# Expert slots in half pairs (68 positions for 71, eight of them split), a slot list in lines of 64 bytes, and routing done a step sooner

## The chip, the cores and the metric

The kernel runs on one core of one Trainium2 chip. The metric is device microseconds (us) from launch to end, the median of several executions. Engines are named as the profile names them: PE (matrix products), PEld (its weight loads), DVE (elementwise work on vectors), ACT (activation functions), POOL (here mostly the issuer of gathers and scatters), SP (an issuer of DMAs). Each engine runs its own instruction list in order and waits on semaphores.

## The reference, cut to what matters

```python
xn = layernorm(x)                                  # x: 2 x 4096 tokens x 256, float32
# deformable attention: 16 heads, 12 samples a query, offsets from a small convolution
g   = gelu(depthwise_conv3(xn @ wq.T + bq))
pos = clip(token + anchor + 6 * tanh(g @ pw_w.T + pw_b), 0, 4095)
k_at, v_at = linear_sample(k, pos), linear_sample(v, pos)
s   = softmax(q . k_at / 4 - rel_scale * |pos - token|) . v_at @ wo.T + bo
# mixture of 8 experts, the best 2 for each token, hidden width 512
p   = softmax(xn @ Wr.T + br);  best 2 of (scores + biases_N), weights p / sum(p of the two)
h   = xn @ Wl1[e] + bl1[e]                         # 256 -> 1024, halves a and b
y_e = (silu(a) * b) @ Wl2[e] + bl2[e]              # 512 -> 256
out = x + s * silu(sum over the two e of weight_e * y_e)
```

8192 tokens with two experts each make 16384 rows of expert work. They are sorted by expert into slots; an expert's last slots may stay empty (they point at rows of zeros behind the tokens).

## The kernel before, in words

**Front** (`front_block`, about 0 to 367 us). First layernorm, V and router scores, tile by tile. Then 16 steps of 512 tokens. In a step PE runs `head_scores` (products of q with nearby keys, four tiles), `project` (q and k of two steps ahead) and `offsets` (the offset products of one step back, two halves into one PSUM tile `pOff`). ACT evacuates, does gelu and tanh and stores. DVE runs `convolve`, `slopes_of_k`, `offset_bias` (frees `pOff`) and `positions`.

Beside the steps DVE does the routing: `choose` (best two) in step 0, `gate_values` and `count_rows` in step 1, `find_slots` and `experts_of_pairs` in step 2; PE's `count_tokens` (sums over tokens) stands at the end of step 1. `find_slots` gives the place of each (token, choice) in a slot list in DRAM. POOL writes that list by 128 indirect DMAs (`scatter`, L556), each 128 elements of 4 bytes, and between their quarters clears the 8 MB that experts add into (`clear_moe`, four DMAs of 2 MB) and loads two experts' first weights (`first_w1`). At the end POOL reads the list back, DVE turns it into token numbers (`inv`, L1157 and L1158), and POOL gathers the first token rows with them.

**Experts** (`mix_block`, to about 1182 us). 71 pairs, each of 2 x 128 slots of one expert. In `period(n)` PE runs `times_w1` twice (into `pA` and `pB`, L1670), `transpose_x` of the next pair (L1664), and `products` of the pair two back (L1723, L1676). ACT applies silu to `pA`, evacuates `pB` and the output. DVE multiplies the two (`gate_hidden`, L1790) between its own 16 steps of attention weights; tables say where (`GATES_AT`), and after which pair or tile ACT does each softmax exponent and its preparation (`EXPONENT_AFTER`, `PREPARE_AFTER`, `END_EXPONENT_AT`, `END_PREPARE_AT`). POOL's `pair_io(n)` loads the weights of pair n+2 (three slots, the third is the tile `bandT`), gathers that pair's token rows (L1379), and `take_y` adds results into DRAM by two scatters (L1398); the scatters of a pair wait for those of the pair before to have landed.

**Tail** (to the end). 64 tiles of 128 tokens: PE transposes bands of attention weights (L1689), multiplies by V (L1704) and by wo (L1714, L1715); SP loads bands, ACT's queue loads V, POOL loads expert sums and writes the output; ACT's `gate_unit` (silu of expert sums) stands at tiles of `END_GATE_AT`, DVE's units of the output at `UNITS_AT` and after the last step. DVE finishes its last steps of attention weights beside it; each of the 16 steps is stored as `band_rows` and feeds four tiles.

Of the kernel before, what the change touches and what calls it, by code (L numbers as in the profile page):

```python
# [30 lines left out]
P = 128  # L31
F32 = mybir.dt.float32
BF16 = mybir.dt.bfloat16
I32 = mybir.dt.int32
# [25 lines left out]
SLOT_PAIRS = TOKENS * TOPK // (2 * P) + EXPERTS - 1  # L60
# [5 lines left out]
LISTED = TOPK * TILES  # L66
COUNT_AT = 1
# [49 lines left out]
STAGE_AT = XS_AT = 2 * KT_PITCH  # L117
ACT_AT = XS_AT + XS_F
# [14 lines left out]
GATES_AT = ((0, 2, 3, 4, 6, 7), (0, 2, 3, 5, 6, 8), (1, 2, 4, 5, 7), (0, 1, 3, 4, 6, 7), (0, 2, 3, 5, 6, 8), (0, 2, 4, 5, 6),  # L133
            (0, 1, 2, 4, 6, 7), (0, 1, 3, 4, 6, 7), (0, 2, 3, 5, 6, 8), (1, 2, 4, 5, 7), (0, 1, 3, 4, 6, 7), (0, 2, 3, 4, 6, 8), (0, 2))
EXPONENT_AFTER = (0, 6, 12, 17, 23, 29, 35, 40, 46, 52, 57, 63, 69)
PREPARE_AFTER = (3, 8, 14, 20, 26, 31, 37, 43, 48, 54, 60, 66)
END_EXPONENT_AT = (6, 24, 42)
END_PREPARE_AT = (1, 14)
END_GATE_AT = (5, 9, 13, 17, 22, 25, 29, 33, 37, 41, 45, 49, 53, 56, 58, 60)
UNITS_AT = ({}, {}, {2: 1, 4: 1, 6: 1}, {0: 1, 2: 1, 4: 1, 6: 1}, {4: 1, 6: 1, 7: 1})  # L140
# [3 lines left out]
def anchors():  # L144

    step = np.arange(SAMPLES, dtype=np.float32) * np.float32(1.0 / (SAMPLES - 1))
    a = np.float32(-RHO) * (np.float32(1) - step) + np.float32(RHO) * step
    a[-1] = RHO
    return [float(v) for v in a]

# [95 lines left out]
def front_block(nc, io, dram, keep):  # L246


    with ExitStack() as ctx:
# [51 lines left out]
        ones = sb("ones", [P, P])  # L301
        rows_i = sb("rows_i", [P, EXPERTS], I32)
        rows = sb("rows", [P, EXPERTS])
        ends = sb("ends", [P, EXPERTS])
        start = sb("start", [P, EXPERTS])
        slot = sb("slot", [P, TOPK, TILES])
        tile_row = sb("tile_row", [1, SLOT_PAIRS])
        tile_exp = sb("tile_exp", [1, SLOT_PAIRS])
        list_f = sb("list_f", [P, HIGH])
        spare_i = sb("spare_i", [P, HIGH], I32)  # L310
        token_i = sb("token_i", [P, TOPK * TILES], I32)
        slot_i = sb("slot_i", [P, TOPK, TILES], U32)
# [26 lines left out]
        pOff = ps("pOff", [P, 512])  # L339
        pCount = ps("pCount", [P, 2 * EXPERTS])  # L340
# [7 lines left out]
        pads_set = sem("pads_set")  # L348
        consts = sem("consts")
# [37 lines left out]
        prefix_ready = sem("prefix_ready")  # L387
        list_set = sem("list_set")
        list_rows = sem("list_rows")
# [3 lines left out]
        keep["front_sx_stored"], keep["front_pads_set"] = sx_stored, pads_set  # L393
        keep["front_stored"] = [(pos_stored[u], 16 * SUBS * (STEPS // 2)) for u in range(2)] + [(sx_stored[u], 16 * STEPS) for u in range(SX_SLOTS)]
        keep["front_stored"] += [(pads_set, 16 * 9), (gates_stored, 16 * 4), (bias_stored, 16)]
# [4 lines left out]
        TAIL = VROWS - TOKENS - REACH  # L400
        HALVES = SUBS // 2
        WEIGHTS = 16 * 7
        ROUTE_WEIGHTS = WEIGHTS + 16 * 5
        CONSTS = 8
# [18 lines left out]
        step = keep["step"]  # L423
        assert XST_AT <= SEQ + 2 and FREE_SLOTS * PAIRS <= SEQ + 2 and PARTS_AT >= XST_AT + KC * PAIR + 3 * TH
# [3 lines left out]
        def _(sp):  # L428
# [94 lines left out]
        def _(pool):  # L523
# [15 lines left out]
            nc.gpsimd.iota(keep["tile_exp"][:], pattern=[[PAIR, SLOT_PAIRS]], base=0, channel_multiplier=0).then_inc(consts, 1)  # L539
# [7 lines left out]
            pool.dma_start(dram["list"].rearrange("(p n) o -> p (n o)", p=P), spare_i[:]).then_inc(list_set, 16)  # L547
# [5 lines left out]
            pool.wait_ge(list_rows, 1)  # L553
# [1515 lines left out]
```

## Time and profile before

| | |
|---|---|
| median of 3 runs | 1437.6 us (1434.17 to 1440.89) |
| the profiled execution | 1440.41 us |
| its span (first to last instruction) | 1438.7 us |
| busy: PE / DVE / ACT / POOL | 1356.0 / 1223.1 / 802.4 / 861.8 us |
| mean granted TensorE clock | 0.976 of full |

A row of a timeline is: start, length, engine, line, operation, output<-inputs, count, and in brackets the idle time before it with what ended it. PE's fp32 matmul shows as two passes: 8 instructions of the program are "x16". A row of windows gives each engine's busy time in a stretch, the granted clock and the share of the DMA engines. Busy is not bound: an engine bounds a stretch where it has no idle time in it or where the others' waits end with it.

### The profile page before, as it was taken

How to read it: one execution, taken by the hardware profiler on the slowest of the kernel's cores; microseconds unless marked ns; L12 is line 12 of the kernel's file. 1: busy time of each engine (PE TensorE's matmuls, PEld its weight loads, DVE VectorE, ACT ScalarE, POOL GpSimd, SP SyncE). 2: the span in 40 equal slices, each digit the busy share in tenths (PEclk: the TensorE clock that was granted, in tenths of full speed). 3: DMA queues.
4: the chain of work that ended last, by engine and by line, in shares of the span. 5: the costliest groups of instructions: out<-in, count | busy, mean ns of one | idle time of the engine just before them, and what ended most of it. 6: DMA issues, size and time to landing. Idle time of an engine off the chain costs nothing. (4 is left out here: it accounts for less than half of the span.)

```text
span 1438.7 us, 35852 instructions
## 1 busy us (share of the span) xinstructions
PE 1356.0 (94%) x13687; PEld 1085.2 (75%) x13687; DVE 1223.1 (85%) x1700; ACT 802.4 (56%) x1873; POOL 861.8 (60%) x566
## 2 busy tenths in 40 slices
PE   5998999997799999999999999999999998899997
PEld 4864565556688888888888888888888886777775
DVE  7846755786899999999999999999999999999361
ACT  2547577777445455545444555545454455665664
POOL 1000377887568888778787877988887746121021
PEclk9999899998899999999999999999999999999999
DMA  7942456886747687775768577677767678999798
GB/s 226 348 166 88 105 161 201 252 258 211 250 134 214 173 233 192 224 225 150 242 141 256 142 229 192 169 223 176 212 153 214 167 169 268 250 267 228 217 275 170
DMA packets 204278, 293.98 MB, mean 204 GB/s; under 512 B 25601, under 2 KB 161029, under 8 KB 203891
## 3 DMA queue, kind: packets, MB, share of 16 engines
q0 software_dynamic: 65792, 146.59, 39.9%
q1 hardware_dynamic: 110723, 133.04, 29.3%
q10 hardware_dynamic: 27632, 12.64, 3.5%
q8 instruction: 79, 1.29, 0.4%
q14 instruction: 52, 0.43, 0.1%
HBM read 182.83 MB, written 117.74 MB: 209 GB/s over the span
## 5 line engine op out<-in xcount | busy, mean ns | idle before, releaser
L1398 POOL DMA_INDIRECT moe_rows<-expert_mem,token_of x142 | 363.3, 2558 | 90.3 <-issue 49.9
L1676 PE MATMUL pY<-expert_mem 128*128 x1136 | 264.2, 386 | 0.0
L1379 POOL DMA_INDIRECT expert_mem<-xn_rows,token_of x138 | 227.7, 1650 | 52.5 <-issue 45.1
L1676 PEld LDWEIGHTS pY<-expert_mem 128*128 128x128 f32 x1136 | 210.0, 190 | 41.8 <-issue 16.1
L1867 DVE SCALAR_TENSOR_TENSOR mid<-pos_pair,mid 128x768 f32<-128x768 f32 x224 | 197.6, 954 | 0.5
L1670 PE MATMUL pA<-mid,expert_mem 128*128 128x256 f32 x768 | 177.4, 385 | 4.4 <-ACT mid L1504 2.7
L1523 ACT ACTIVATE expert_mem<-pA,b1sel 128x256 f32<-128x256 f32 x284 | 111.2, 474 | 122.9 <-issue 122.7
L556 POOL DMA_INDIRECT slot_list<-token_i,high_part x128 | 141.0, 1101 | 58.2 <-issue 38.7
L1670 PE MATMUL pB<-mid,expert_mem 128*128 128x256 f32 x768 | 173.6, 379 | 0.0
L1532 ACT ACTIVATE expert_mem<-pB,b1sel 128x256 f32<-128x256 f32 x284 | 111.5, 475 | 109.2 <-PE pB L1670 109.2
L219 DVE SCALAR_TENSOR_TENSOR mid<-mid 128x768 f32<-128x768 f32 x192 | 169.6, 952 | 0.0
L1670 PEld LDWEIGHTS pA<-mid,expert_mem 128*128 128x128 f32 x768 | 148.2, 193 | 25.9 <-issue 5.2
L1670 PEld LDWEIGHTS pB<-mid,expert_mem 128*128 128x128 f32 x768 | 145.9, 190 | 19.8
L1543 ACT ACTIVATE expert_mem<-pY,gsel 128x256 f32<-128x256 f32 x142 | 59.6, 470 | 155.4 <-PE pY L1676 155.4
L783 PE MATMUL pQK<-mid,wqk 128*128 128x512 f32 x256 | 125.3, 635 | 1.4 <-ACT mid L639 0.8
L1440 POOL DMA_DIRECT2D out<-expert_mem x15 | 19.4, 1298 | 164.1 <-DVE expert_mem L1889 163.8
L1790 DVE TENSOR_TENSOR expert_mem<-expert_mem 128x1024 f32<-128x1024 f32 x71 | 87.0, 1225 | 25.1 <-ACT expert_mem L1532 23.1
L803 PEld LDWEIGHTS pS<-expert_mem,qm 32*64 32x64 f32 x4096 | 55.9, 138 | 50.5 <-issue 46.2
L1930 DVE TENSOR_TENSOR mid<-mid 128x5376 f32<-128x5376 f32 x16 | 92.1, 5758 | 0.6
L783 PEld LDWEIGHTS pQK<-mid,wqk 128*128 128x128 f32 x256 | 48.9, 200 | 56.0 <-issue 51.8
L551 POOL DMA_DIRECT2D xn_rows<-scores x4 | 4.6, 1159 | 136.5 <-DVE scores L989 136.5
L803 PE MATMUL pS<-expert_mem,qm 32*64 32x47 f32 x4096 | 65.8, 244 | 18.7 <-issue 10.3
(223 smaller groups left out, 2546.6 us busy)
## 6 DMA issues: line engine op xcount, KB each, us to landing
expert_mem<-in_w_l POOLq DMA_DIRECT2D x48, 1024.0 KB, 7.7
band<-band_rows SPq DMA_DIRECT2D x256, 96.0 KB, 3.1
S_rows<-expert_mem SPq DMA_DIRECT2D x64, 376.0 KB
bandT<-in_w_l POOLq DMA_DIRECT2D x23, 1024.0 KB, 7.1
band_rows<-wgt SPq DMA_DIRECT2D x12, 1536.0 KB, 7.2
pos_pair<-pos_rows SPq DMA_DIRECT2D x28, 384.0 KB, 7.9
xn_rows<-expert_mem SPq DMA_DIRECT2D x16, 512.0 KB, 5.5
v_rows<-expert_mem SPq DMA_DIRECT2D x16, 512.0 KB, 4.3
```

Source lines behind the costliest of these rows:

```text
L219: return V.scalar_tensor_tensor(in_rows(self.parts[:, slot]), self.posT.rearrange("p r b t -> p r (b t)"), float(i + 1 - REACH), each_row( ...
L556: nc.gpsimd.indirect_dma_start(out=dram["list"], out_offset=bass.IndirectOffsetOnAxis(ap=list_row[:, c:c + 1], axis=0), in_=token_i[:, c:c ...
L783: mm = nc.tensor.matmul(pQK[:, c], wqk[:, k, first:first + P], qT[:, k, qcol(m):qcol(m) + GTOK], start=(k == 0), stop=(k == KC - 1))
L803: mm = nc.tensor.matmul(pS[s % 2 * 2 * SUB:(s % 2 + 1) * 2 * SUB, g, col:col + SKEYS], qm[rows, a // 2, c, a % 2 * SUBS + s].rearrange("p ...
L1379: nc.gpsimd.indirect_dma_start(out=xs[:, u, s], out_offset=None, in_=dram["xn"], in_offset=bass.IndirectOffsetOnAxis(ap=keep["inv"][:, 2 * ...
L1398: nc.gpsimd.indirect_dma_start(out=dram["moe"], out_offset=bass.IndirectOffsetOnAxis(ap=keep["inv"][:, 2 * n + s:2 * n + s + 1], axis=0), ...
L1523: ins = nc.scalar.activation(act_a[:, u, c], pA[:, c], ACT.Silu, bias=b1sel[:, u, c:c + 1])
L1532: ins = nc.scalar.activation(hid[:, h, c], pB[:, c], ACT.Identity, bias=b1sel[:, u, HC + c:HC + c + 1])
L1670: mm = nc.tensor.matmul(dst[:, c], w1_slots[w1_slot(n)][:, k, o * HID + c * P:o * HID + (c + 1) * P], xsT[:, k], start=(k == 0), stop=(k = ...
L1676: mm = nc.tensor.matmul(pY[:, s], hid[:, h, c, s * P:(s + 1) * P], w2[:, c, ds(e * D, D)], start=False, stop=(s == 1 and c == HC - 1))
L1867: ins = V.scalar_tensor_tensor(parts[:, j], at, float(j - REACH), prob, ALU.max, ALU.mult)
L1930: chain(V.tensor_tensor(pair_terms[:, :, 0], pair_terms[:, :, 0], pair_terms[:, :, 1], ALU.add))
```

## The change

1. **Half pairs.** Slots are filled in halves of 128. An expert with an odd number of halves gives its last half to one of eight positions at which two experts share a pair. 60 whole pairs and 8 split positions make 68 (the last of them holds one half only). Seven split pairs (4, 13, 22, ..., 58) run `times_w1` four times on 128 columns, with two loads of weights, two bias products, 128-wide ACT work, and a second scatter that waits for the first.
2. **List lines.** A slot's entry is a line of 16 floats (64 bytes). The cleared list is built in the upper part of `kT`, stored at the start and read back there.
3. **Sooner routing.** `choose` and `count_rows` in step 0, `count_tokens` behind the first score tile of step 1, `gate_values` and `find_slots` (now 34 operations for 17) before the offsets of step 1. `pOff` has two banks, so `offsets` waits for an evacuation one half further back; the counts lie in the second bank.
4. **Queues.** `clear_moe` goes from POOL to SP, 16 DMAs of 512 KB, one in each step. The rows of zeros are stored at the start. SP loads the first bands before the store of weights that stood ahead of them.
5. **Tables** for 68 pairs; three exponents beside the tail become four.

```diff
-SLOT_PAIRS = TOKENS * TOPK // (2 * P) + EXPERTS - 1
+HALF_SLOTS = TOKENS * TOPK // P + EXPERTS - 1
+WHOLE_PAIRS = (TOKENS * TOPK // P - EXPERTS) // 2
+SPLIT_PAIRS = (HALF_SLOTS - 2 * WHOLE_PAIRS + 1) // 2
+SLOT_PAIRS = WHOLE_PAIRS + SPLIT_PAIRS
+RUN, SPLIT_AT = 8, 4
+LINE = 16
...
-EXPONENT_AFTER = (0, 6, 12, 17, 23, 29, 35, 40, 46, 52, 57, 63, 69)
-END_EXPONENT_AT = (6, 24, 42)
-END_GATE_AT = (5, 9, 13, 17, 22, 25, 29, 33, 37, 41, 45, 49, 53, 56, 58, 60)
-UNITS_AT = ({}, {}, {2: 1, 4: 1, 6: 1}, {0: 1, 2: 1, 4: 1, 6: 1}, {4: 1, 6: 1, 7: 1})
+EXPONENT_AFTER = (0, 6, 12, 17, 23, 28, 34, 40, 45, 51, 57, 62)
+END_EXPONENT_AT = (2, 18, 35, 50)
+END_GATE_AT = (8, 11, 14, 17, 21, 25, 29, 33, 37, 41, 45, 49, 53, 56, 58, 60)
+UNITS_AT = ({}, {6: 1, 8: 1}, {0: 1, 2: 1, 4: 1, 6: 1}, {0: 1, 2: 1, 5: 1}, {})
...
+            def clear_moe(q):
+                sp.dma_start(dram["moe"][rows_of(q), :].rearrange("(t p) c -> p t c", p=P),
+                             zeros[:, None, :].broadcast_to([P, GROUP, D])).then_inc(moe_cleared, 16)
...
+            nc.gpsimd.tensor_copy(lines, spare_i[:].unsqueeze(2).broadcast_to([P, HIGH, LINE])).then_inc(lines_set, 1)
+            pool.wait_ge(lines_set, 1)
+            pool.dma_start(dram["list"].rearrange("(p n) l -> p n l", p=P), lines).then_inc(list_set, 16)
...
-                        in_=token_i[:, c:c + 1], in_offset=None).then_inc(scattered, 16)
+                        in_=token_f[:, c:c + LINE], in_offset=None).then_inc(scattered, 16)
...
             pool.wait_ge(scattered, 16 * LISTED)
-            pool.dma_start(spare_i[:], dram["list"].rearrange("(p n) o -> p (n o)", p=P)).then_inc(list_loaded, 16)
+            pool.wait_ge(s_done, LINES_GROUP * GROUP + 1)
+            pool.dma_start(lines, dram["list"].rearrange("(p n) l -> p n l", p=P)).then_inc(list_loaded, 16)
...
             def offsets(n, h):
                 pe.wait_ge(gel_ready, n + 1)
-                if 2 * n + h > 0:
-                    pe.wait_ge(off_ready, 2 * n + h)
+                if 2 * n + h > 1:
+                    pe.wait_ge(off_ready, 2 * n + h - 1)
+                if 2 * n + h == 1:
+                    pe.wait_ge(counts_taken, 1)
...
             dve.wait_ge(list_loaded, 16)
-            chain(V.tensor_copy(list_f[:], spare_i[:]))
-            V.tensor_scalar(keep["inv"][:], list_f[:], float(TOKENS), None, ALU.add).then_inc(tokens_known, 1)
+            V.tensor_scalar(keep["inv"][:], lines[:, :, 0], float(TOKENS), None, ALU.add).then_inc(tokens_known, 1)
...
+            def buffer_free(use):
+                return {2: 1, 4: 2}.get(use, use - 2)
+            def loads_in(n):
+                done = [k for k in range(1, SLOT_PAIRS)]
+                return [use for use in range(2, len(W1_USES)) if use != LAG + 1 and
+                        n == min(k for k in done if FIRST_USE[k] >= buffer_free(use))]
...
-                for s in range(2):
+                for s in range(halves(n)):
+                    if is_split(n) and s == 1:
+                        pool.wait_ge(ys_stored[u], 32 * (n // 2) + 16)
+                        pool.sem_inc(go, 1)
                     nc.gpsimd.indirect_dma_start(
                         out=dram["moe"], ...
...
-                pe.wait_ge(w1_loaded[w1_slot(n)], 16 * w1_loads(n))
                 pe.wait_ge(xsT_ready, n + 1)
-                if not first:
-                    pe.wait_ge(a_ready, n)
-                times_w1(pA, n, 0).then_inc(a_done, 1)
-                if not first:
-                    pe.wait_ge(b_ready, n)
-                times_w1(pB, n, 1).then_inc(b_done, 1)
+                for part, use in enumerate(uses_of(n)):
+                    cols = slice(part * P, (part + 1) * P) if is_split(n) else slice(0, PAIR)
+                    pe.wait_ge(w1_loaded[w1_slot(use)], 16 * w1_loads(use))
+                    if n > 0:
+                        pe.wait_ge(a_ready, n)
+                    times_w1(pA, use, 0, cols).then_inc(a_done, 1)
+                    if n > 0:
+                        pe.wait_ge(b_ready, n)
+                    times_w1(pB, use, 1, cols).then_inc(b_done, 1)
```

On PE, in the experts: a whole pair of the kernel before (`pA`, `pB` are the two halves of the hidden layer, `pX` the next pair's transposes, `pY` the output).

```order
L1670 MATMUL pA<-mid,expert_mem 128x256 x8
L1670 MATMUL pB<-mid,expert_mem 128x256 x8
L1664 MATMUL pX<-ident,expert_mem 128x128 x4
L1656 TENSOR_LOAD tile_exp_i
L1656 ISA x2
L1723 ISA
L1723 MATMUL pY<-b,ones 128x512
```

And a split pair of the kernel after, at the same place of a period.

```order
L1784 MATMUL pA<-mid,expert_mem 128x128 x8
L1784 MATMUL pB<-mid,expert_mem 128x128 x8
L1784 MATMUL pA<-mid,bandT 128x128 x8
L1784 MATMUL pB<-mid,bandT 128x128 x8
L1778 MATMUL pX<-ident,expert_mem 128x128 x4
L1770 TENSOR_LOAD tile_exp_i
L1770 ISA x2
```

The same 256 columns pass in twice as many instructions of half the width, with two weight tiles (`expert_mem` and `bandT` here); the rest of the period stands as it did.

On POOL, in the experts: one `pair_io` of the kernel before, a weight load, two gathers and two scatters.

```order
L1385 TENSOR_LOAD tile_exp_i [waits b_done]
L1385 ISA x2
L1388 ISA
L1388 DMA expert_mem<-in_w_l 128x2x1024
L1379 DMA expert_mem<-xn_rows,token_of 128x264 [waits xsT_done,gate_taken]
L1379 DMA expert_mem<-xn_rows,token_of 128x264
L1398 DMA moe_rows<-expert_mem,token_of 8448x256 [waits ys_ready,ys_stored1]
L1398 DMA moe_rows<-expert_mem,token_of 8448x256
```

After, the one whose scatters belong to a split pair, and the load behind them.

```order
L1473 TENSOR_LOAD tile_exp_i [waits b_done]
L1473 ISA x2
L1477 ISA
L1477 DMA expert_mem<-in_w_l 128x2x1024
L1467 DMA expert_mem<-xn_rows,token_of 128x264 [waits xsT_done,gate_taken]
L1467 DMA expert_mem<-xn_rows,token_of 128x264
L1500 DMA moe_rows<-expert_mem,token_of 8448x256 [waits ys_ready,ys_stored0]
L1500 DMA moe_rows<-expert_mem,token_of 8448x256 [waits ys_stored1]
L1473 TENSOR_LOAD tile_exp_i [waits b_done]
```

The second scatter has a wait of its own, and the next pair's weight load is queued behind it.

On DVE, in step 1 of the front, before the change: the first evacuation of offsets (`off<-pOff`, L935) ahead of the gate values (`scores`) and the counts by expert (`total`).

```order
L910 TENSOR_TENSOR expert_mem<-expert_mem 128x2x512
L935 TENSOR_TENSOR off<-pOff,pw_b 128x384
L985 TENSOR_TENSOR slope<-expert_mem 128x512
L986 TENSOR_TENSOR scores<-pos_pair,slope 128x512
L987 TENSOR_REDUCE top<-scores 128x64
L988 RECIPROCAL top<-top 128x64
```

After, at the end of that step's routing (the last operations of `find_slots`, then both evacuations, then the experts of the pairs).

```order
L1102 SCALAR_TENSOR_TENSOR slot<-list_f,slot 128x128
L1103 SCALAR_TENSOR_TENSOR slot<-list_f,slot 128x128
L1104 SCALAR_TENSOR_TENSOR slot_high<-slot_high,slot 128x128
L1105 SCALAR_TENSOR_TENSOR high_part<-slot_low,slot_high 128x128
L998 TENSOR_TENSOR off<-pOff,pw_b 128x384 x2
L1110 TENSOR_SCALAR odds<-odds,ends 128x8
L1111 TENSOR_SCALAR tile_exp<-tile_row,ends 1x136
```

Both evacuations moved behind all of `find_slots`, which itself begins with a wait for PE's `count_tokens`.

## Rows read from the trace of the kernel before

**Rows 1.** Windows: stretch, length, busy PE PEld DVE ACT POOL, clock, DMA share, GB/s.
```profile
0.00:108.00 108.00, 89.50 (x413) 69.73 (x414) 73.57 (x333) 45.29 (x89) 4.43 (x18) 1.00 0.76 247
108.00:367.00 259.00, 227.05 (x4584) 145.13 (x4582) 180.15 (x363) 186.34 (x364) 159.08 (x146) 0.92 0.59 182
400.00:1140.00 740.00, 740.00 (x3469) 630.05 (x3468) 710.18 (x727) 376.77 (x980) 603.18 (x327) 1.00 0.71 195
1182.00:1438.00 256.00, 229.48 (x4912) 182.14 (x4910) 188.09 (x196) 158.07 (x359) 59.87 (x54) 0.97 0.93 238
```

**Rows 2.** Timeline of PE, one pair of the experts and the next's start.
```profile
1137.95 3.62 PE L1670 MATMUL pA<-mid,expert_mem 128*128 128x256 f32 x16
1141.41 3.62 PE L1670 MATMUL pB<-mid,expert_mem 128*128 128x256 f32 x16
1149.27 3.62 PE L1670 MATMUL pA<-mid,bandT 128*128 128x256 f32 x16
```

**Rows 3.** Lines by form, PE's weight loads: busy, mean ns of one, idle before.
```profile
L1670 PEld LDWEIGHTS pB<-mid,expert_mem 128*128 128x128 f32 x768 | 145.9, 190 | 19.8
```

**Rows 4.** Chain of waits, tail: transposes of two tiles, 128 columns a pass.
```profile
1348.17 1.04 PE pA L1689 x8
...
1355.25 1.04 PE pA L1689 x8
```

**Rows 5.** Costliest groups of the page: POOL's scatters and gathers.
```profile
L1398 POOL DMA_INDIRECT moe_rows<-expert_mem,token_of x142 | 363.3, 2558 | 90.3 <-issue 49.9
L1379 POOL DMA_INDIRECT expert_mem<-xn_rows,token_of x138 | 227.7, 1650 | 52.5 <-issue 45.1
```

**Rows 6.** DMA issues: count, KB each, median us from issue to landing.
```profile
expert_mem<-in_w_l POOLq DMA_DIRECT2D x48, 1024.0 KB, 7.7
...
band_rows<-wgt POOLq DMA_DIRECT2D x4, 1536.0 KB, 11.4
...
moe_rows<-expert_mem,token_of POOLq DMA_INDIRECT x142, 4.6
```

**Rows 7.** Timelines: PE's second product of pair 7, end of the period.
```profile
451.43 3.62 PE L1670 MATMUL pB<-mid,expert_mem 128*128 128x256 f32 x16
```

**Rows 8.** Timeline of POOL: the weight load that waits for it.
```profile
463.81 1.36 POOL L1388 DMA_DIRECT2D expert_mem<-in_w_l  x1
```

**Rows 9.** Timeline of PE in the front and the first pairs: waits.
```profile
143.96 0.52 PE L822 MATMUL pCount<-total,below 128*128 128x8 f32 x2 [3.39 <-DVE total L995]
...
338.22 2.51 PE L815 MATMUL pOff<-pw_w,conv 128*128 128x192 f32 x8 [1.76 <-DVE off L935]
...
361.75 2.15 PE L815 MATMUL pOff<-pw_w,conv 128*128 128x192 f32 x8 [2.49 <-DVE off L935]
...
367.08 1.08 PE L1664 MATMUL pX<-ident,expert_mem 128*128 128x128 f32 x4 [3.17 <-DMA expert_mem<-xn_rows,token_of]
...
389.66 5.38 PE L1670 MATMUL pA<-mid,expert_mem 128*128 128x256 f32 x16 [1.91 <-ACT mid L1504]
```

**Rows 10.** Timeline of DVE: the list is read back.
```profile
360.63 0.23 DVE L1157 CAST list_f<-spare_i 128x142 f32<-128x142 int32 x1 [3.90 <-DMA spare_i<-slot_list]
```

**Rows 11.** One line's instructions: POOL's list scatters, min/median/max ns, from to.
```profile
L556 POOL DMA_INDIRECT slot_list<-token_i,high_part x128: 965/972/2503, 166.7 to 351.9; - x128
```

**Rows 12.** Timeline of PE: the tail begins, and its first long wait.
```profile
1181.85 1.31 PE L1704 MATMUL pB<-bandT,vk 96*32 96x32 f32 x64
...
1211.59 1.34 PE L1704 MATMUL pB<-bandT,expert_mem 96*32 96x32 f32 x64 [6.08 <-ACT bandT L1550]
```

**Rows 13.** Timeline of DVE: last step of attention weights, from its wait to its end.
```profile
1354.64 0.56 DVE L1844 TENSOR_TENSOR mid<-mid 128x384 f32<-128x384 f32 x1 [22.69 <-ACT mid L1599]
...
1386.30 1.29 DVE L1947 TENSOR_TENSOR wgt<-gslope 128x1088 f32<-128x1088 f32 x1
```

**Rows 14.** Chain of waits, end: the last wait for a band, the last PE release.
```profile
1366.46 7.47 DMA band<-band_rows
...
1430.09 0.39 ACT expert_mem L1576
```

More of the change, by code:

```diff
@@ L149, in anchors, with is_split, halves, uses_of @@
     return [float(v) for v in a]
+def is_split(n):
+    return n % (RUN + 1) == SPLIT_AT
+def halves(n):
+    return 1 if n == SLOT_PAIRS - 1 else 2
+def uses_of(n):
+    return range(FIRST_USE[n], FIRST_USE[n + 1])
+def w1_slot(use):
+    return use if use < 2 else (0, 2, 1)[(use - 2) % W1_SLOTS]
+def w1_loads(use):
+    return sum(w1_slot(m) == w1_slot(use) for m in range(use + 1))
 def in_rows(ap):
@@ L983, in gate_values @@
             def gate_values():
-                dve.wait_ge(exp_out, 1)
-                chain(V.tensor_tensor(count, chosen[0], chosen[1], ALU.add))
                 chain(V.tensor_tensor(scores[:], expw, count, ALU.mult))
@@ L991, in count_rows @@
             def count_rows():
+                dve.wait_ge(exp_out, 1)
+                chain(V.tensor_tensor(count, chosen[0], chosen[1], ALU.add))
                 for e in range(EXPERTS):
@@ L1368, in _ @@
                 fill_out(it)
+            for n in range(BAND_SLOTS):
+                tile_in(n)
             store_weights(BY_SP - 1)
@@ L1371, in _ @@
             reload_slope(BY_SP + 2)
-            for n in range(TILES):
+            for n in range(BAND_SLOTS, TILES):
                 tile_in(n)
@@ L1403, in pair_io @@
             def pair_io(n, u, first=False, left=SLOT_PAIRS):
-                ahead = n + 1 if n < LAG else n + 2
-                if not first and ahead < SLOT_PAIRS:
-                    pool.wait_ge(b_done, n)
+                if not first and loads_in(n):
+                    pool.wait_ge(b_done, FIRST_USE[n])
                     pool.sem_inc(go, 1)
-                    load_w1(ahead)
+                    for use in loads_in(n):
+                        load_w1(use)
                 if left > 2:
@@ L1518, in silu, with cols_of @@
+                ins.then_inc(gate_taken, 1)
+            def cols_of(n, part):
+                return slice(part * P, (part + 1) * P) if is_split(n) else slice(0, PAIR)
+            def silu(n, u):
                 act.wait_ge(gate_taken, n + 1)
[L1519 to L1520 removed]
+                if n >= 2:
                     act.wait_ge(hid_ready, n - 1)
[L1522 to L1523 removed]
+                act.wait_ge(a_done, FIRST_USE[n + 1])
+                for part in range(len(uses_of(n))):
+                    for c in range(HC):
+                        ins = nc.scalar.activation(act_a[:, u, c, cols_of(n, part)], pA[:, c, cols_of(n, part)], ACT.Silu,
+                                                   bias=b1sel[:, u, part, c:c + 1])
@@ L1524, in silu @@
                 ins.then_inc(a_ready, 1)
             def evacuate_b(n, h, u):
-                act.wait_ge(b_done, n + 1)
-                if not (isinstance(n, int) and n < HSLOTS):
+                if n >= HSLOTS:
                     act.wait_ge(y_done, n - HSLOTS + 1)
-                for c in range(HC):
-                    ins = nc.scalar.activation(hid[:, h, c], pB[:, c], ACT.Identity, bias=b1sel[:, u, HC + c:HC + c + 1])
+                act.wait_ge(b_done, FIRST_USE[n + 1])
+                for part in range(len(uses_of(n))):
+                    for c in range(HC):
+                        ins = nc.scalar.activation(hid[:, h, c, cols_of(n, part)], pB[:, c, cols_of(n, part)], ACT.Identity,
+                                                   bias=b1sel[:, u, part, HC + c:HC + c + 1])
```

251 lines of the change are left out of this document (151 added, 100 removed).

## The prediction

> **What bounds the kernel now.** I read the windows first, one for each stage [rows 1]. From 400 to 1140 us PE is busy 740.00 of 740 us: the experts are bound by PE without a gap, and whatever PE is spared there comes off the end. DVE (710.18) and POOL (603.18 and the gaps between its operations) are close behind, so both have to be priced as the next bound. From 108 to 367 PE is busy 227.05 of 259 at a granted clock of 0.92: the front is short waits in turn. From 1182 on PE has 229.48 of 256 and the DMA engines 0.93: the tail is PE with waits for transfers. Then I read the timelines: one pair on PE [rows 2], POOL's distance behind PE [rows 7, 8], the waits of the front [rows 9, 10], and what ends last, DVE's last step and the band made of it [rows 13, 14].
>
> All sums stand against the profiled execution, 1440.4 us (span 1438.7 and 1.7 around it). The median of the runs shown is 1437.6, 2.8 less, and I take these 2.8 off at the end.
>
> **The experts: 71 pairs become 68 positions.** A period is 1149.27 - 1137.95 = 11.32 us, of which `pA` and `pB` take 3.46 each, start to start, for 16 passes of 256 columns: 0.216 a pass [rows 2]. The last position holds one half, so 67.5 periods stand for 71: 3.5 x 11.32 = 39.6 us less. (The lone half saves a little less than half, since its weights are loaded all the same.)
>
> The seven split pairs issue 64 passes of 128 columns for 32 of 256. The trace has no such product in the experts. Nearest are the transposes of the tail, 8 passes of 128 columns in 1.04 us [rows 4], 0.13 a pass with fresh data; half of 0.216 is 0.108. The other end is the weight load of a pass, 190 ns of busy time [rows 3]: if a load can't hide beside a pass this short, each pass takes 0.19. I take 0.12, between the first two, because those are measured start to start and the load's own length isn't: 64 x 0.12 = 7.7 for 6.9, and 0.3 for the second bias product, about 1.0 a split, 7 us over seven. The ends are 0 and 64 x 0.19 + 0.3 - 6.9 = 5.6 a split, 0 to 39 in all.
>
> On this the Trainium skill speaks against the change ("TensorE: Matmul & The Clock Gate", sections "LDWEIGHTS (loading the stationary operand)" and "The mechanism"): a load costs its columns over 1.2 in ns, 107 for 128 columns by the page, and runs beside a matmul in flight only when the row groups differ, which for full-height weights they don't. By that rule each pass would be its columns and the load, which would add over 40 us and make the change a loss. The trace speaks against the rule: 16 passes with 16 loads take 3.46 us [rows 2], which leaves no room for 16 times 190 ns [rows 3] in series.
>
> ACT's 16 instructions of half width instead of 8 and DVE's unchanged `gate_hidden` lie beside PE: ACT is busy 376.77 of 740 [rows 1]. If a split's evacuation came late, PE would wait one or two ACT instructions, part of the +-.
>
> POOL's work for a pair is two scatters of 2.56, two gathers of 1.65 [rows 5] and a load; the window gives 603.18 / 65.4 periods = 9.2 us busy [rows 1], and five gaps of 0.3 between operations make 10.7 of 11.32. A split adds a weight load of 1.36 [rows 8] with a gap, and the landing of the first scatter before the second may be issued, 4.6 us by the median [rows 6], in all some 6.3. POOL then lags, and wins back 0.6 a pair, 5.4 until the next split. So a lag of about 1 us stays from each split. It matters only where a load is needed soon: ahead of a split pair three slots hold only 15.7 us from the freeing product to the pair that needs the load (11.32 and the 4.4 of a period that follows `pB`), of which 7.7 is the landing [rows 6] and 0.8 the issue. 7.2 are left to lag in. Today's lag is at most 463.81 - (451.43 + 3.62) = 8.8 [rows 7, 8], seldom over 4. I give 3 us of PE waits for it. Experts: -39.6 + 7 + 3 = -29.6.
>
> **The front.** Scatters run from 166.7 to 351.9 [rows 11] and the list is read back at 360.63 after a wait of 3.90 [rows 10]; DVE stands still there with `offset_bias` queued behind, and PE waits 2.49 for the offsets and 3.17 for the first gathered rows [rows 9]. With routing one step earlier (about 15 us) the list is ready before its reader, so these go; what is late next is the step's own chain through ACT's tanh. The second bank of `pOff` takes away the 1.76 of the kind at 338.22 [rows 9]. Together 7.4. Against it: the count's 3.39 [rows 9] becomes another wait, since 34 small operations and a wait for PE's counts now stand ahead of both evacuations of step 1, with ACT's tanh and the positions queued behind; I call that even, +-4. The early store of list lines (1.1 MB) and pads (0.5 MB) at the 247 GB/s of that stretch is 6.5 us of DMA time at most [rows 1], most of it under layernorm work, cost 0.5. `clear_moe` on SP moves the same 8 MB; its 16 issues stand between stores that have slack, nothing. The lines read back (1.1 MB instead of 70 KB) land over 15 us ahead of their use. Front: -7, bounds -14 and +4.
>
> **The tail.** The experts' last product ends at 1181.85 [rows 12]; less 7 and 29.6 this is about 1145. Work of DVE does not shrink by as much: it loses three `gate_hidden`, 3.7 us, and the front's 7. So its last step moves later against PE. Before, the last exponent stood behind tile 42 and DVE waited 22.69 for it, going on at 1354.64, 172.8 after the tail's begin [rows 13]. Now it stands behind tile 50: eight tiles of 3.54 later (two tiles from 1348.17 to 1355.25 [rows 4]), less some 4.6 of the wait of 6.08 for an expert sum [rows 12], whose reader moves from tile 5 to 8: 196.5, so 1341.7. DVE would be there at about 1321 (1331.95 less 10.7), so it waits for ACT's turn again. The step took 1387.5 - 1354.64 = 32.9 [rows 13] with three units of 1.2 that now stand elsewhere, so 29.5: weights at 1371, the store 11.4 [rows 6], the band 7.5 [rows 14]: 1390. PE then has the last four tiles and the end: 4 x 3.54 + 8.6 (1430.09 to 1438.7 [rows 14]) = 1413. Without this hold PE would finish about 11 sooner, 1402. So of the 37 us won, the tail gives back 11.
>
> **Sum.** Span 1413, 1414.7 with what lies around it, less 2.8: 1412.
>
> **Rivals.**
> - *The tail isn't held.* If the last band lands before PE comes to it, the 11 us don't go: 1401. For it: the store of 11.4 and the landing of 7.5 were timed beside a DMA share of 0.93 [rows 1] and may be shorter at the very end. Against: PE would reach tile 60 at 1341.7 + 10 x 3.54 = 1377, and the chain above is 13 later.
> - *POOL becomes the bound.* 67.5 x 10.7 = 722, and for each split 6.3 to 9.4 (a landing as slow as a weight load's, 7.7 for 4.6 [rows 6]): 766 to 788 for PE's 771. The middle of what exceeds, 9: 1421.
> - *Passes of 128 columns go by their loads.* 0.19 each [rows 3]: 32 more than in the sum, 1443, no change. For it: PEld is busy 630 of 740 [rows 1]. Against: rows 4.
> - *Slower: PE stalls at each split.* If POOL is as late as 8.8 [rows 7, 8] when a split's extra load is due and has some 3.5 of a landing left to wait for, the weights come 5 after they are needed; and after a wait PE ran its next 16 passes in 5.38 for 3.62 [rows 9], another 1.8. 6.8 at each of seven splits is 48 us: 1460. It decides from 4.7 us a split on, where seven have eaten the gain of 25.6 and the 7.2 of the bound below. For it: POOL has only 0.6 of slack a pair. Against: lags of that size are rare, and the tables for loads give a use three slots.
> - *The routing change costs more than it wins* (front +4 or worse, the rest as forecast): 1423.
>
> **How the numbers follow.** A measurement of this kernel can tell 0.5%, 7.2 us: same is 1430.4 to 1444.8. Forecast 0.50 (1412; its own range 1403 to 1421), tail not held 0.14 (1401), POOL bound 0.18 (1421), loads 0.08 (1443), stalls 0.06 (1460), routing and the rest 0.04. Faster: all of the first three, and half of the last: 0.84. Same: the loads' case and an edge of POOL's: 0.09. Slower: the stalls and an edge of the loads': 0.07. The range leaves out the two slow cases and the far end of the second: 1395 to 1435.
>
> **What would show it.** Right: whole periods of 11.3 us, split ones of 12.3 with no idle time on PE; the experts end near 1145; DVE waits some 20 us for the last exponent at about 1342, and PE waits near 1377 to 1390 for a band. Wrong: split periods of 16 or more (loads), idle time on PE ahead of `pA` released by a weight DMA (POOL), PE waits in steps 1 and 2 of the front of more than 10 us together, or no wait at tile 60.

## The result and the profile after

The kernel after takes 1425.0 us (median of 19 runs, 1419.2 to 1487.7; one of them, disturbed, is left out of the comparison), the kernel before 1437.9 beside it: ratio 0.9913, interval 0.9898 to 0.9928. It is faster by 12.9 us where 25.6 were forecast: the sign was right, the size half. The time lies inside the range, beyond the forecast's own (1403 to 1421).

The profiled execution is one of 1424.97 us, span 1423.3. First its windows, cut at like stages as [rows 1] (columns as there), and two short stretches of the tail.

```profile
0.00:108.00 108.00, 89.46 (x413) 69.69 (x414) 73.54 (x335) 45.25 (x89) 8.87 (x25) 1.00 0.79 261
108.00:361.00 253.00, 226.38 (x4593) 144.60 (x4592) 189.41 (x393) 185.45 (x366) 154.62 (x139) 0.93 0.63 194
395.00:1120.00 725.00, 723.84 (x3603) 619.75 (x3602) 697.59 (x717) 376.43 (x1025) 590.03 (x319) 1.00 0.72 204
1139.70:1170.00 30.30, 18.70 (x378) 14.67 (x378) 29.77 (x33) 11.53 (x25) 17.72 (x7) 0.77 0.88 230
1370.00:1410.00 40.00, 17.54 (x347) 13.46 (x348) 14.46 (x16) 11.44 (x25) 11.45 (x10) 0.70 0.90 201
```

In the experts PE was busy 723.84 of 725 us, as asked. The last two rows are where the forecast went wrong: 18.70 busy of 30.30 as the tail begins, 17.54 of 40 near its end, with a mean granted clock of 0.77 and 0.70.

The experts on PE: a split pair, the start of the whole pair behind it and of the next (answering to [rows 2]).

```profile
404.65 1.95 PE L1784 MATMUL pA<-mid,expert_mem 128*128 128x128 f32 x16
...
410.01 1.95 PE L1784 MATMUL pB<-mid,expert_mem 128*128 128x128 f32 x16
...
416.20 3.62 PE L1784 MATMUL pA<-mid,bandT 128*128 128x256 f32 x16
...
427.51 3.62 PE L1784 MATMUL pA<-mid,expert_mem 128*128 128x256 f32 x16
```

From 404.65 to 416.20 is 11.55, against 11.31 for the whole pair behind it: 0.24 more, 1.79 for 16 passes of 128 columns, 0.112 a pass. The second bias product costs another 0.3 two periods later. So this split costs 0.54, where 1.0 was forecast. Three others cost as much and two 0.8; at the one left, PE waited besides (1.16).

The front on PE and DVE (answering to [rows 9, 10]), and POOL's gathers behind it.

```profile
152.57 1.22 PE L864 MATMUL pS<-expert_mem,qm 32*64 32x47 f32 x64 [6.00 <-ACT expert_mem L722]
...
358.32 0.63 PE L1778 MATMUL pX<-ident,expert_mem 128*128 128x128 f32 x4 [2.62 <-DMA expert_mem<-xn_rows,token_of]
```
```profile
351.20 0.27 DVE L1248 TENSOR_SCALAR token_of<-expert_mem 128x136 uint32<-128x136 f32 x1
```
```profile
352.31 0.99 POOL L654 DMA_INDIRECT expert_mem<-xn_rows,token_of  x1 [15.99 <-DVE token_of L1248]
```

The waits of 1.76, 2.49 and 3.90 are gone and the 3.17 is 2.62. The count's 3.39 came back as 6.00 behind ACT, as forecast. The experts begin at 358.32 for 367.08. The list now waits for DVE, not DVE for the list: POOL stood 15.99 us until DVE had read it.

The tail on PE, DVE and SP (answering to [rows 12, 13]): PE's waits, DVE's last step, and SP's list from its second group of bands on.

```profile
1139.70 1.29 PE L1818 MATMUL pB<-bandT,vk 96*32 96x32 f32 x64
1143.62 0.68 PE L1803 MATMUL pBT<-ident,band 128*96 128x128 f32 x4 [2.63 <-DMA band<-band_rows]
...
1160.87 1.09 PE L1803 MATMUL pBT<-ident,band 128*96 128x128 f32 x4 [8.97 <-DMA band<-band_rows]
...
1395.26 1.09 PE L1803 MATMUL pBT<-ident,band 128*96 128x128 f32 x4 [22.04 <-DMA band<-band_rows]
```
```profile
1347.73 0.56 DVE L1965 TENSOR_TENSOR mid<-mid 128x384 f32<-128x384 f32 x1 [19.04 <-ACT mid L1713]
...
1375.98 1.29 DVE L2068 TENSOR_TENSOR wgt<-gslope 128x1088 f32<-128x1088 f32 x1
```
```profile
1137.35 3.64 SPq L1436 DMA_DIRECT2D band<-band_rows  x4
...
1144.89 0.58 SPq L1413 DMA_DIRECT2D band_rows<-wgt  x1
...
1146.15 8.28 SPq L1397 DMA_DIRECT2D slope<-S_rows  x8
...
1155.17 4.95 SPq L1436 DMA_DIRECT2D band<-band_rows  x8
```

The new waits are 2.63 and 8.97 for the bands of tiles 2 and 4 at the tail's begin, and 22.04 for the band of tile 60, the first that DVE's last step feeds. In the kernel before no wait for a band after its last weights (1387.5 [rows 13]) was over 0.7.

The 8.97 comes out of SP's list: the band of tile 4 stands there behind the store of weights and the reload of slopes, 10.3 us of issues from 1144.89 on. In the kernel before both stood 24 us and more ahead of the tail's begin at 1181.85:

```profile
1148.45 0.39 SPq L1327 DMA_DIRECT2D band_rows<-wgt  x1
...
1151.12 5.80 SPq L1311 DMA_DIRECT2D slope<-S_rows  x8
```

Store and reload follow DVE's weights of step 11. DVE finished these only 13 us sooner, where PE came to the tail 42 us sooner (before, then after):

```profile
1147.13 1.29 DVE L1947 TENSOR_TENSOR wgt<-gslope 128x1088 f32<-128x1088 f32 x1
```
```profile
1133.93 1.29 DVE L2068 TENSOR_TENSOR wgt<-gslope 128x1088 f32<-128x1088 f32 x1
```

Besides, SP stood 41.0 us ahead of tile 2's loads until POOL had cleared their buffer at 1136.0. In the kernel before that wait was 2.5, and SP's bands of tile 2 were issued 12.6 us ahead of the tail instead of 2.4.

The chain that ended last tells what the 22.04 is made of.

```profile
1346.85 0.85 ACT mid L1713
...
1378.06 7.34 DMA band_rows<-wgt
...
1388.67 6.46 DMA band<-band_rows
...
1398.43 2.01 PE pY L1828 x4
...
1414.58 0.39 ACT expert_mem L1690
```

ACT's exponent behind tile 50 ends near 1347.7, DVE's step (rows above) at 1377.3, the store of the weights near 1385, the band at 1395.1, and only then PE goes on. Its next product with `wo` takes 2.01, start to start, where 1.06 is usual.

### The profile page after: what moved, and what is told of

Its sections match the earlier page's. It is cut to its first block and busy times, and to the rows that moved or that the text cites. A ratio compares the mean times of both kernels' runs of the same rounds, so it can differ in the third digit from the quotient of the medians.

```text
span 1423.3 us, 36091 instructions
## 1 busy us (share of the span) xinstructions
PE 1319.1 (93%) x13749; PEld 1057.9 (74%) x13749; DVE 1226.3 (86%) x1725; ACT 794.0 (56%) x1902; POOL 850.3 (60%) x556
## 5 line engine op out<-in xcount | busy, mean ns | idle before, releaser
L1500 POOL DMA_INDIRECT moe_rows<-expert_mem,token_of x135 | 332.3, 2462 | 107.9 <-issue 68.9
L1467 POOL DMA_INDIRECT expert_mem<-xn_rows,token_of x131 | 243.8, 1861 | 45.6 <-issue 36.5
L1790 PE MATMUL pY<-expert_mem 128*128 x1080 | 253.1, 386 | 0.0
L1790 PEld LDWEIGHTS pY<-expert_mem 128*128 128x128 f32 x1080 | 199.0, 190 | 39.4 <-issue 13.6
L1634 ACT ACTIVATE expert_mem<-pA,b1sel 128x256 f32<-128x256 f32 (+1 forms) x300 | 110.1, 455 | 128.8 <-PE pA L1784 125.9
L1784 PE MATMUL pA<-mid,expert_mem 128*128 128x256 f32 (+1 forms) x816 | 169.9, 362 | 5.6 <-ACT mid L1606 4.4
L626 POOL DMA_INDIRECT slot_list<-token_f,high_part x128 | 143.3, 1119 | 46.8 <-issue 46.8
L1784 PE MATMUL pB<-mid,expert_mem 128*128 128x256 f32 (+1 forms) x816 | 166.1, 357 | 0.0
L1645 ACT ACTIVATE expert_mem<-pB,b1sel 128x256 f32<-128x256 f32 (+1 forms) x300 | 110.6, 466 | 96.1 <-PE pB L1784 96.1
L1784 PE MATMUL pA<-mid,bandT 128*128 128x256 f32 (+1 forms) x384 | 80.2, 362 | 0.0
```

Source lines behind the costliest of these rows:

```text
L626: nc.gpsimd.indirect_dma_start(out=dram["list"], out_offset=bass.IndirectOffsetOnAxis(ap=list_row[:, c:c + 1], axis=0), in_=token_f[:, c:c ...
L1467: nc.gpsimd.indirect_dma_start(out=xs[:, u, s], out_offset=None, in_=dram["xn"], in_offset=bass.IndirectOffsetOnAxis(ap=keep["inv"][:, 2 * ...
L1500: nc.gpsimd.indirect_dma_start(out=dram["moe"], out_offset=bass.IndirectOffsetOnAxis(ap=keep["inv"][:, 2 * n + s:2 * n + s + 1], axis=0), ...
L1634: ins = nc.scalar.activation(act_a[:, u, c, cols_of(n, part)], pA[:, c, cols_of(n, part)], ACT.Silu, bias=b1sel[:, u, part, c:c + 1])
L1645: ins = nc.scalar.activation(hid[:, h, c, cols_of(n, part)], pB[:, c, cols_of(n, part)], ACT.Identity, bias=b1sel[:, u, part, HC + c:HC + ...
L1784: mm = nc.tensor.matmul(dst[:, c, cols], w1_slots[w1_slot(use)][:, k, o * HID + c * P:o * HID + (c + 1) * P], xsT[:, k, cols], start=(k == ...
```

## The experiments

All compare with runs of the kernel before on the same chip; the kernel after stands at 0.9913 by its own. Rows are of the timelines of each, unless said otherwise.

**The last exponent four tiles sooner.**

```diff
-END_EXPONENT_AT = (2, 18, 35, 50)
+END_EXPONENT_AT = (2, 18, 35, 46)
```

> The kernel after, with the last softmax exponent behind tile 46 instead of 50. Theory A (the tail's end is set by the place of the last exponent, and DVE's wait of 19.04 us for it): PE passes tile 46 about 14 us sooner than tile 50, so DVE's wait falls to about 5, PE's wait of 22.04 for the last band to about 8, and the kernel is 10 to 16 us faster than the kernel after, some 1411. Rival B (the tail goes at the pace of the DMA engines or of DVE's other steps): within 3 us of the kernel after, 1425. Rival C (ACT stalls in front of tile 47, since DVE isn't ready): PE gains a wait of over 5 us near tile 48 and at most half of the 14 comes through.

Measured: 1410.0, ratio 0.9814 (0.9791 to 0.9837), some 14 us better than after. DVE and PE in it:

```profile
1330.73 0.56 DVE L1965 TENSOR_TENSOR mid<-mid 128x384 f32<-128x384 f32 x1 [4.85 <-ACT mid L1713]
```
```profile
1378.92 1.09 PE L1803 MATMUL pBT<-ident,band 128*96 128x128 f32 x4 [9.07 <-DMA band<-band_rows]
```

DVE's wait went from 19.04 to 4.85, PE's from 22.04 to 9.07: theory A, with its numbers. No other edit tried beats this one.

**Four tiles later.** The same line with 54.

> The kernel after with its last exponent behind tile 54, the suspected cost made larger. Theory A: DVE's wait of 19.04 and PE's of 22.04 both grow by four tiles, 14 us, and the kernel is 13 to 15 us slower than after, about the time of the kernel before (ratio 0.998 to 1.003). Rival B (the DMA engines or DVE's units pace the tail): under 5 us slower.

Measured: 1.0015 (0.9992 to 1.0038), theory A: the whole gain of the change gone, by one number in a table.

```profile
1375.02 0.56 DVE L1965 TENSOR_TENSOR mid<-mid 128x384 f32<-128x384 f32 x1 [36.22 <-ACT mid L1713]
```
```profile
1422.59 1.09 PE L1803 MATMUL pBT<-ident,band 128*96 128x128 f32 x4 [36.15 <-DMA band<-band_rows]
```

46, 50 and 54 lie about 14 us apart each: four tiles of 3.54. In this execution POOL was late once at a split (a scatter at 600.09 took 6.30 us):

```profile
616.06 1.40 POOL L1477 DMA_DIRECT2D expert_mem<-in_w_l  x1
```
```profile
613.13 2.05 PE L1784 MATMUL pA<-mid,expert_mem 128*128 128x128 f32 x16 [1.22 <-DMA expert_mem<-in_w_l]
...
626.89 5.82 PE L1784 MATMUL pA<-mid,expert_mem 128*128 128x256 f32 x16 [5.52 <-issue]
```

The weight load for the next pair was issued at 616.06, and PE stood 5.52 and then ran that pair's first 16 passes in 5.82 for 3.62. The profile names nothing that released the 5.52, so POOL as its cause is read from the order of the issues and not shown. It looks like the prediction's slow rival, at one split of seven in one execution. The profile of after has one such wait, of 1.16, and that of the run with the reload on POOL two of 1.6.

**Two tiles sooner still.** The same line with 44.

> The kernel after with its last exponent behind tile 44. DVE is ready for it at about 1326 and ACT reaches it at about 1321. Theory A (from here DVE's own work sets the end, so the step of 3.5 us a tile stops): 2 to 5 us better than behind tile 46 (ratio 0.9814 there), ACT and PE lose some 3 to 5 us near tile 46 that PE's wait of 9.07 ahead of the last band covers; PE's last wait falls to 2 to 6. Rival B (still tied to the tile): 7 us better. Rival C (ACT's stall costs PE in full): no better, or worse.

Measured: 1415.9, 0.984 (0.9812 to 0.9868), no better than 46: rival C on time. ACT now waits for DVE, and PE for ACT:

```profile
1335.20 1.32 PE L1818 MATMUL pB<-bandT,expert_mem 96*32 96x32 f32 x64 [2.87 <-ACT bandT L1664]
...
1379.36 1.09 PE L1803 MATMUL pBT<-ident,band 128*96 128x128 f32 x4 [3.55 <-DMA band<-band_rows]
...
1387.31 0.68 PE L1803 MATMUL pBT<-ident,band 128*96 128x128 f32 x4
```

DVE's wait is 0.91 there, and the slope of 3.5 us a tile has ended. The 3.55 is for the band of tile 58, not for the last: PE begins the transposes of tile 60 (1387.31) without a wait. So the chain exponent, step, store, band no longer holds the end. The chain that ended last now goes through DVE's work to 1333.3 and ACT (1334.19) to PE's wait of 2.87, and from there along PE. DVE's work still sets the end, but through ACT's stall at tile 46, and that takes back what the last band gave.

**The kernel before, with its exponent sooner.**

```diff
-END_EXPONENT_AT = (6, 24, 42)
+END_EXPONENT_AT = (6, 24, 38)
```

> The kernel before, with its last exponent behind tile 38 instead of 42. There DVE waited 22.69 us for it too, but PE came to the last band only 0.6 us early or late. Theory A (in the kernel before the place of the exponent hid behind PE's own pace; only the shorter experts uncovered it): DVE's wait falls to about 8 and the time stays within 3 us of the kernel before. Rival B (the kernel before was held as well): 8 to 14 us faster.

Measured: 0.9991 (0.9976 to 1.0006), no change, though DVE's wait fell from 22.69 [rows 13] to 7.76:

```profile
1336.41 0.56 DVE L1844 TENSOR_TENSOR mid<-mid 128x384 f32<-128x384 f32 x1 [7.76 <-ACT mid L1599]
```

So a wait of the same kind, and of like length (22.69 and 19.04), cost nothing before and 14 us after: theory A.

**SP's order at the tail's begin.**

```diff
-            for n in range(BAND_SLOTS):
+            for n in range(2):
                 tile_in(n)
             store_weights(BY_SP - 1)
             load_pos(BY_SP)
+            for n in range(2, 2 * BAND_SLOTS):
+                tile_in(n)
             reload_slope(BY_SP + 2)
-            for n in range(BAND_SLOTS, TILES):
+            for n in range(2 * BAND_SLOTS, TILES):
```

> The kernel after, with SP's list at the begin of the tail reordered: first bands of two tiles, then the store of step 11 of the weights, then the bands up to tile 7, then the reload of slopes (after: bands of four tiles, store, reload, the rest). Theory A (the reload and the wait of tile 2's band stand ahead of tile 4's, and the exponents are tied to tiles, so PE's delay moves the end): PE's waits of 2.63 and 8.97 near 1143 and 1161 fall to under 4 together, the tail's tiles and the last exponent come 6 to 9 us sooner and so does the end, 1417. Rival B (DVE's pace sets the end, PE only waits elsewhere): the 8.97 goes, a wait as long shows at the last band, the time is that of the kernel after within 2 us.

Measured: 1432.1, 0.9954 (0.993 to 0.9979), some 6 us worse than after: both theories fell. The 2.63 grew to 6.36, and the 8.97 is not gone but stands four tiles later:

```profile
1138.74 1.09 PE L1805 MATMUL pBT<-ident,band 128*96 128x128 f32 x4 [6.36 <-DMA band<-band_rows]
...
1170.12 1.08 PE L1805 MATMUL pBT<-ident,band 128*96 128x128 f32 x4 [9.23 <-DMA band<-band_rows]
```

**Both edits** (46 became 48).

> Both edits, with the last exponent behind tile 48 (PE being sooner by about 8 us there). Theory A: DVE's wait for it is 3 to 8 us, PE's for the last band under 10, time 1405 to 1412: faster than either edit alone. Rival B: no better than the better of the two alone.

Measured: 0.9862 (0.9835 to 0.9889), some 1419, no better than the exponent alone: rival B. Theory A of that run fell.

**The reload on POOL's queue.**

```diff
             load_pos(BY_SP)
-            reload_slope(BY_SP + 2)
...
             for k in range(MOE_AHEAD):
                 load_moe(k)
+            reload_slope(LAST - 1)
```

The first hunk is SP's, the second POOL's; who waits for it counts accordingly.

> The kernel after, with the reload of slopes for step 14 (8 DMAs and one of positions, 8 us of SP's list between the bands of tiles 3 and 4) issued by POOL behind its first loads of expert sums. Theory A (this reload, once 25 us ahead of the tail and now in it, holds tile 4's band): PE's wait of 8.97 near 1161 falls under 2, the last exponent, tied to tile 50, comes 6 to 9 us sooner and so does the end: 6 to 9 us faster than the kernel after, some 1417. Rival B (PE would only wait for the next band, since SP issues bands hardly faster than PE uses them): the waits spread over tiles 4 to 20 and add to as much, no change.

Measured: 0.9929 (0.9902 to 0.9955), no change. The 8.97 is 4.09, but other waits follow, one of them for ACT:

```profile
1137.06 1.29 PE L1818 MATMUL pB<-bandT,vk 96*32 96x32 f32 x64
...
1153.55 1.09 PE L1803 MATMUL pBT<-ident,band 128*96 128x128 f32 x4 [4.09 <-DMA band<-band_rows]
...
1191.20 1.31 PE L1818 MATMUL pB<-bandT,expert_mem 96*32 96x32 f32 x64 [3.43 <-ACT bandT L1664]
```
```profile
1343.25 0.56 DVE L1965 TENSOR_TENSOR mid<-mid 128x384 f32<-128x384 f32 x1 [19.49 <-ACT mid L1713]
```

From the tail's first product to DVE going on is 206.2, in after 1347.73 - 1139.70 = 208.0. Rival B: taking one transfer out of SP's list gives 2 us, not 8. What paces the first 20 tiles besides it stays open; several transfers and ACT's sum are late by turns.

**The same with the exponent behind 48.**

> The same and the last exponent behind tile 48. Theory A: DVE is ready for it near 1328 whatever PE does, so this gives what the exponent behind tile 46 alone gave, 1408 to 1412, since DVE's own work then sets the end. Rival B (PE's place sets it in any case): some 6 us better than that, 1403.

Measured: 1422.0, 0.9883 (0.9861 to 0.9905): some 7 us better than the same with 50 (0.9929), two tiles at 3.5, but worse than 46 without the reload moved. DVE still waited 11.02. Theory A's 1408 to 1412 was not reached, nor rival B's 1403.

**Offsets ahead of the slot list in step 1.**

```diff
-                dve.wait_ge(prefix_ready, 1)
-                V.tensor_copy(counts[:], pCount).then_inc(counts_taken, 1)
...
                 if n == COUNT_AT:
+                    dve.wait_ge(prefix_ready, 1)
+                    V.tensor_copy(counts[:], pCount).then_inc(counts_taken, 1)
+                    offset_bias(0, 0)
+                    offset_bias(0, 1)
                     gate_values()
                     find_slots()
-                if n > 0:
+                if n > 0 and n != COUNT_AT:
...
```

The first lines stood in `find_slots`; the condition, which is changed for both halves, keeps the evacuations from being done twice.

> The kernel after, with DVE in step 1 evacuating both halves of the offsets (after copying the counts) ahead of the gate values and the slot computation. Theory A (routing ahead of the evacuations holds ACT's tanh 7.95 and by it PE 6.00 us near 152): that wait of PE falls under 2, the experts begin 3 to 5 us sooner, and the kernel is 0 to 5 us faster, less if the exponents' places take it back. Rival B (the wait only moves to step 2, since DVE has the same work): waits of PE in steps 1 and 2 stay within 2 us of 8 together, no change.

Measured: 1436.9, 0.9978 (0.9957 to 0.9999), 9 us worse than after. Both A and B fell:

```profile
171.36 1.06 ACT L730 ACTIVATE conv<-conv 128x1024 f32<-128x1024 f32 x1 [17.18 <-DVE conv L992]
```
```profile
173.31 1.22 PE L864 MATMUL pS<-expert_mem,qm 32*64 32x47 f32 x64 [16.55 <-ACT expert_mem L722]
```

DVE now stood idle 4.73 and 1.75 us for PE's offsets ahead of the 34 operations, and `convolve` of step 2 came behind them; ACT's gelu waited 17.18 for it and PE 16.55. The routing ahead of the evacuations fills time in which DVE would have waited.

**One bank for the offsets.**

```diff
-                if 2 * n + h > 1:
-                    pe.wait_ge(off_ready, 2 * n + h - 1)
-                if 2 * n + h == 1:
-                    pe.wait_ge(counts_taken, 1)
+                if 2 * n + h > 0:
+                    pe.wait_ge(off_ready, 2 * n + h)
...
-                        mm = nc.tensor.matmul(pOff[:, h, a * HR:(a + 1) * HR], ...
+                        mm = nc.tensor.matmul(pOff[:, 0, a * HR:(a + 1) * HR], ...
```

DVE's evacuation reads bank 0 accordingly; the counts stay in the other bank.

> The kernel after with one bank for the offsets: each half waits for the evacuation of the half before, as in the kernel before. Theory A (the second bank takes away PE's waits of 1.7 to 2.5 for DVE's evacuations at the end of the front, and in step 1 lets PE go on while DVE is in the slot computation): waits for DVE's evacuation come back, 1 to 2.5 each near 330 to 355 and some 8 to 10 in step 1 in place of the 6.00, and the experts begin 4 to 9 us later. Rival B (ACT's tanh and scores hold PE in any case): within 2 us of the kernel after.

Measured: 1434.8, 0.9976 (0.9958 to 0.9994): without its second bank the change wins next to nothing. Theory A:

```profile
154.28 2.90 PE L876 MATMUL pOff<-pw_w,conv 128*128 128x192 f32 x8 [9.86 <-DVE off L996]
...
337.52 1.54 PE L876 MATMUL pOff<-pw_w,conv 128*128 128x192 f32 x8 [1.71 <-DVE off L996]
```

The 6.00 for ACT became 9.86 for DVE, the waits of the end came back, and the experts began at 365.52.

**The list read sooner**, on top of the exponent behind 46 and behind 44 (the two lines that wait for the list and make `inv` moved ahead of `offset_bias(STEPS - 2, 0)`).

> The kernel after with the last exponent behind tile 46, and DVE's reading of the slot list two evacuations of offsets sooner (it stood ready some 10 us before DVE came to it, and PE waits 2.62 for the first gathered rows). Theory A: PE's wait ahead of the experts falls under 0.5, the experts begin 2 to 3 us sooner, the time is 0 to 3 us better than with the exponent alone (1410). Rival B: DVE waits for the list there by 1 us or more, and PE gains that wait at the last offsets: no change or worse.

> The last exponent behind tile 44 and the slot list read two evacuations sooner, as in the run with 46. Theory A: the 2 to 3 us ahead of the experts come through only in part, since DVE's work up to its last exponent, not PE, then sets the end: 0 to 3 us better than behind tile 44 alone. Rival B: all of it is lost, or the two together are slower than the exponent alone.

Measured: 0.9836 (0.9802 to 0.9869) and 0.984 (0.9815 to 0.9865), the same as the exponents alone: no gain is shown, though one of 0 to 3 us would be hard to see in these intervals. The 2.62 for the gathered rows is 0.78 in the run with 46. It is gone in the run with 44, where PE waits 3.04 for ACT instead:

```profile
357.89 3.72 PE L1784 MATMUL pA<-mid,expert_mem 128*128 128x256 f32 x16 [3.04 <-ACT mid L1606]
```

## Why the prediction was half right

- **Experts: right, and a little better.** From PE's first transposes to the tail's first product it was 781.4 us for 814.8: 33.4 less for 29.6 forecast. A split cost 0.54 to 0.8 for 1.0, and PE waited 1.16 at one of them where 3 in all were forecast for POOL.
- **Loads of a pass: the rival fell.** 0.112 a pass is about half of 0.216, so 128 more columns cost 0.104, which leaves 0.008 for a load in series. With a load's busy time still at 190 ns the loads lie beside the products, at 128 columns too. The rule of the Trainium skill ("TensorE: Matmul & The Clock Gate", "The mechanism"), as the prediction took it, that a load runs beside a product only when the row groups differ, disagrees with this: 16 passes with 16 loads took 1.79 us. The same section also lets a load into a background weight buffer go ahead of products in flight, and with this the trace agrees; which buffer a load went to, no run shows.
- **Front: right in size.** 8.8 sooner for 7. Of the named waits the 1.76 and the 2.49 went, and the 3.17 only became 2.62; all of PE's waits from 108 us to the begin of the experts fell from 31.9 to 25.9. The second bank was named for the waits near 338 only; the run with one bank shows that it carries step 1 too, some 9 us in all.
- **DVE's last step and the store: right.** 29.5 from its wait's end to the weights, as forecast; 18.0 on to the band for 18.9.
- **The tail's 196.5: the step that failed.** The forecast took a wait of 6.08 as mostly gone and put nothing in its place. Measured from the first product of the tail to DVE going on: 208.0, 11.5 more. The 6.08 did go. But PE's waits over 0.3 us from there to the exponent's tile come to 22.1 us, where the sum stands for the 15.5 of the kernel before less 4.6. 11.6 of the 22.1 are for bands that weren't there (2.63 and 8.97), with a lower clock behind (0.77 in that stretch). The forecast did say that DVE's work shrinks less than PE's, but used it for DVE's last step alone. SP's store and reload are tied to DVE too: they came 13 us sooner, PE 42, and so they fell into the tail's begin. SP's first bands, moved ahead of the store by the change, have no term in the sum. The runs with SP's order and with the reload on POOL show that this is not one transfer's doing: without it others take most of its place.
- **The last four tiles: 14.2 became 19.3.** The chain counts the band from the transposes of tile 60, but the products run a tile behind, so five tiles of products were left; and PE came out of its 22.04 us at the lower clock (0.57 from 1395.2 to 1401.8).
- **The hold itself: right in kind.** The chain exponent, step, store, band set the end, as the forecast said, and the exponent's place gives 3.5 us a tile (46, 50, 54) until DVE isn't ready (44). The wait was too small, 13 for 22.04: PE came to tile 60 at 1373.2 for 1377, the band at 1395.3 for 1390. The price in time was put at 11 us and is 10 to 14 (exponent behind 44 or 46). What no run reached is the end of 1401 without a hold: with 46 (1410) PE still waits 9.07, and with 44 (1415.9), where the last band holds nothing, ACT's stall has taken its place.
- The sum from 1413 to 1423.3: front and experts -5.5, exponent +11.5, store and band -0.9, last tiles +5.3. The 2.8 between profile and median, taken off at the end, did not hold for the kernel after, whose profiled execution is its median; which execution was profiled is chance.
- **Slips in the working.** POOL's lag in the kernel before was not "at most" 8.8 and "seldom over 4": it reaches 9.6 (load at 656.92, product's end at 643.72 + 3.62) and is over 4 at 22 of 66 loads, so the case against stalls was weaker than it read. The loads' case is 1412 + 32 = 1444, not 1443. The "over 40 us" takes the 190 ns of [rows 3]: 7 x 32 x 0.19 = 42.6. With the 107 ns of the Trainium skill ("TensorE: Matmul & The Clock Gate", "LDWEIGHTS (loading the stationary operand)") the estimate is 24, and by it the change would not have been a loss.

POOL as the bound and the untouched tail (1421 and 1401) did not happen; the first, and the 1423 for a front that costs more than it wins, came near the measured time by luck, for another reason.

## What to carry to other kernels

When one engine's stretch gets shorter, look at what is tied by position to that engine's progress and at what is tied to another's: a wait of 22 us that cost nothing became the end of the kernel when PE came 40 us sooner, and one number in a table gave 14 us back. When a wait is taken off in the sum, ask of every queue that feeds the same point what it will be doing at the new, earlier time. An order that looks like a delay (the routing ahead of the offsets) may fill another wait: try it before calling it a cost.

## What the runs showed of the hardware

- The lower clock behind a wait didn't need 22 us of it. Behind the 9.07 of the run with 46 the granted clock was 0.50 (the lower level, 1.2 GHz) from 1378.9 to 1384.2, and PE's first product with `wo` took 2.08, as behind the 22.04. Behind the 2.63 of the kernel after it was 0.64 from 1143.6 to 1148.3, and that product took 2.08 too (the run with 46, then after):

```profile
1382.05 2.08 PE L1828 MATMUL pY<-wo,mid 128*128 128x256 f32 x4
```
```profile
1145.92 2.08 PE L1828 MATMUL pY<-wo,mid 128*128 128x256 f32 x4
```

In the run with 44 the clock was 0.50 behind the 2.87. Behind the 3.55 it was 0.50 for two transposes, then 0.89 over the next 5.8 us, and the product with `wo` took 1.13. So the length of one wait alone doesn't tell how long the lower clock lasts (windows, columns as in [rows 1]; the clock is the third number from the end):

```profile
1335.20:1340.70 5.50, 5.50 (x81) 3.97 (x82) 5.36 (x9) 5.33 (x11) 0.00 (x0) 0.50 0.89 286
1379.30:1381.30 2.00, 1.94 (x12) 1.53 (x16) 0.00 (x0) 0.59 (x1) 1.23 (x1) 0.50 1.16 286
```

- The same front began the experts at 353.9 to 362.9 us in the profiled executions of seven kernels that share it, and the front of the kernel before at 367.1 and, in the run with 38, at 363.7. In the two that began last (361.1 and 362.9) the granted clock was 0.93 from 108 to 250 us and 0.98 from 250 to 320; in the two that began first (353.9 and 354.2) it was 0.95 and 1.00. The spread is as much as the front's whole gain, so a single pair of profiles doesn't measure that gain well; the means, 357.6 and 365.4, give 7.8. Whether the clock is the cause of the spread is not shown.
